# A fused six-block kernel: value copies moved to DVE, two normalisations to ACT, transposes moved ahead of the projection

## The reference

```
x += 0.5*tanh(LN(x) W1 W2 W3 + b);  x += linear_attention(LN(x))     # 16 heads
x += 0.5*tanh(LN(x) W1 W2 W3 + b);  x += 0.5*(real(ifft(fft(LN(x)) w)) + b)
h  = LN(x)                                                         # softmax block
for each of 16 heads:  q, k, v = h Q, h K, h V                      # 64 wide
                       y = softmax(causal(q k^T / 128)) v;  z += y W / 16
x += z;   x += 0.5*(real(ifft(fft(LN(x)) w)) + b)                   # "z" block
```

## Time and profile before

| what | value |
|---|---|
| median of 3 runs (lowest, highest) | 1288.23 us (1285.64, 1289.4) |
| the profiled execution's own time | 1286.5 us |
| its span, first to last instruction | 1284.8 us |
| mean granted clock of PE | 0.990 |
| busy: PE, PEld, DVE, ACT, POOL | 1211.6, 1047.2, 995.5, 1031.6, 591.3 us |
| batch loop | from about 260 us to the end |

### The profile page before, as it was taken

The page is one execution under the profiler, slowest core; times in us unless marked ns, Lnnn a source line. Parts: engine busy times, 40 slices in busy tenths (PEclk is TensorE's granted clock), DMA queues, the critical chain, the costliest instruction groups (busy, mean ns, idle before and its releaser), DMA issues.

```text
span 1284.8 us, 38257 instructions
## 1 busy us (share of the span) xinstructions
PE 1211.6 (94%) x10883; PEld 1047.2 (82%) x10883; DVE 995.5 (77%) x4814; ACT 1031.6 (80%) x3554; POOL 591.3 (46%) x913
## 2 busy tenths in 40 slices
PE   5799977899999999999999999999999999999996
PEld 4688966778788888888888888888888888888885
DVE  6888879877777777777777777777777777777774
ACT  4866657588788888888888888888888888888883
POOL 4722248534444444444444444444444444444442
PEclk9999999999999999999999999999999999999998
DMA  8000000000000000000000000000000000000000
GB/s 218 1 2 0 1 1 1 1 2 2 3 10 0 8 0 8 0 8 0 8 0 8 0 8 0 8 0 8 0 8 0 8 0 8 0 8 0 9 2 17
DMA packets 14444, 11.81 MB, mean 9 GB/s; under 512 B 852, under 2 KB 12664, under 8 KB 14200
## 3 DMA queue, kind: packets, MB, share of 16 engines
q1 hardware_dynamic: 14240, 11.19, 3.2%
q10 hardware_dynamic: 152, 0.00, 0.0%
HBM read 7.00 MB, written 4.19 MB: 9 GB/s over the span
## 4 chain that ended last, share of the span: by engine, by line
PE 70%; ACT 14%; issue 8%; DVE 3%; POOL 2%; DMA 1%; ACTq 1%; SPq 1%; POOLq 0%; DVEq 0%
PE ps L1145 14%; PE ps L1154 9%; ACT pr L799 7%; PE ps L1128 7%; PE ps L1110 5%; PE ps L1097 5%; PE ps L1114 5%; PE ps L1098 4%; PE ps L1099 4%; ACT qk_hi L784 3%; PE ps L975 2%; PE ps L997 2%; ACT pT L808 1%; PE ps L1136 1%; PE ps L1134 1%
## 5 line engine op out<-in xcount | busy, mean ns | idle before, releaser
L799 ACT ACTIVATE pr<-ps,neg_max 128x128 f32<-128x128 f32 (+1 forms) x1024 | 427.7, 435 | 103.3 <-DVE neg_max L536 103.3
L333 POOL TENSOR_TENSOR pr<-pr,rinv 128x256 f32<-128x256 f32 x256 | 157.9, 617 | 539.8 <-DVE rinv L544 539.8
L536 DVE CUSTOM_DVE_ANT_0 ps<-ps,mask 128x128 f32<-128x128 f32 (+1 forms) x1024 | 329.7, 391 | 0.2
L335 POOL TENSOR_TENSOR pr<-pr,rinv 128x512 f32<-128x512 f32 x256 | 266.5, 1041 | 0.0
L551 DVE COPY pT<-ps 128x512 f32<-128x512 f32 x256 | 175.5, 686 | 97.9 <-PE ps L1128 95.5
L799 ACT ACTIVATION_READ_ACCUMULATOR pr<-ps,neg_max 128x1 f32 x1024 | 222.1, 217 | 0.0
L1128 PE MATMUL ps<-ident,pr 128*128 128x128 f32 x1536 | 211.0, 273 | 2.2 <-POOL pr L335 0.9
L1128 PEld LDWEIGHTS ps<-ident,pr 128*128 128x128 f32 x1536 | 179.9, 141 | 20.9 <-POOL pr L335 2.2
L1145 PE MATMUL ps<-pT,space 128*64 128x256 f32 (+1 forms) x2048 | 196.1, 334 | 0.7 <-ACT pT L808 0.5
L1145 PEld LDWEIGHTS ps<-pT,space 128*64 128x64 f32 x2048 | 127.4, 137 | 56.2 <-ACT pT L808 0.8
L1097 PE MATMUL ps<-x_hi,wqk_hi 128*128 128x256 f32 x512 | 168.5, 329 | 2.8 <-issue 2.3
(11 more groups left out here) (187 smaller groups left out, 2659.7 us busy)
## 6 DMA issues: line engine op xcount, KB each, us to landing
out<-x_all SPq DMA_DIRECT2D x16, 256.0 KB, 2.3
x_all<-L_attn_x SPq DMA_DIRECT2D x1, 768.0 KB, 6.2
x_all<-L_attn_x SPq DMA_DIRECT2D x1, 512.0 KB, 4.0
space<-L_attn_Q SPq DMA_DIRECT2D x1, 512.0 KB, 15.3
space<-L_attn_K SPq DMA_DIRECT2D x1, 512.0 KB, 9.5
space<-L_attn_V SPq DMA_DIRECT2D x1, 512.0 KB, 11.3
space<-L_attn_W SPq DMA_DIRECT2D x1, 512.0 KB, 11.7
dft_s<-dft SPq DMA_DIRECT2D x1, 192.0 KB, 2.6
```

The lines of the kernel that those rows point to most:

```text
L333: nc.gpsimd.tensor_tensor(pr[:, buf, :, 0, :], pr[:, buf, :, 0, :], r[:, :, 0:1].to_broadcast([P, 2, P]), ALU.mult)
L335: nc.gpsimd.tensor_tensor(pr[:, buf, :, 1:3, :].rearrange("p h b k -> p h (b k)"), pr[:, buf, :, 1:3, :].rearrange("p h b k -> p h (b k)") ...
L536: last = nc.vector.tensor_tensor_reduce(o, o, mask[:, T - w:T], -1.0, -MASKED, ALU.add, ALU.min, neg_max[:, j, 2 * h + qt:2 * h + qt + 1])
L799: last = nc.scalar.activation(dst, ps[:, BANK_S + 2 * j + h, qt * P:qt * P + w], ACT.Exp, bias=neg_max[:, j, at:at + 1], scale=-1.0, accum ...
```

## The change

- DVE makes the copies of the even turns' value products (`values_copy`: quarter 2 in turn 0, quarter 0 of the next batch in turn 6), with the same semaphore `v_ready`; ACT keeps those of the odd turns.
- ACT makes both normalisations of the batch loop, as `x*rstd + shift`, behind its second pT copy and ahead of the even pair's exponentials; POOL gets two small products for each (-mean and shift), DVE a wait for POOL's shift ahead of the statistics.
- In turn 2 PE makes the transposes ahead of the projection, z's first, and ACT copies x's transpose ahead of `qk_whole`; z's stays behind it. DVE's `x_low` gets a wait for `z_xT_ready` of an earlier batch.
- Ahead of the loop and behind it the same moves are made; the first norm stands ahead of ACT's copies of the q and k weights.

```diff
@@ declarations (rest left out) @@
+        act_pause = sb("act_pause", [P, 3])
+        z_neg = sb("z_neg", [P, BT]); z_shift = sb("z_shift", [P, BT])
+        z_shift_ready = sem("z_shift_ready")
@@ -307,19 +307,17 @@
             def inv_std(n, j, w):
 
                 pool.wait_ge(mv_ready, count(n + 1))
+                if w == GT and above_0(n - 1):
+                    pool.wait_ge(xn_ready, count(n - 1))
                 if above_0(n - 1):
-                    pool.wait_ge(xn_ready, count(n - 1))
-                if w == GT and above_0(n - 1):
                     pool.wait_ge(xn_act_ready, count(n - 1))
-                if w == GT:
-                    nc.gpsimd.tensor_tensor(neg_mean[:, j, :], mv[:, j, :, 0], minus_1[:], ALU.mult).then_inc(neg_mean_ready, 1)
+                nc.gpsimd.tensor_tensor(neg_mean[:, j, 0:w], mv[:, j, 0:w, 0], minus_1[:, 0:w], ALU.mult).then_inc(neg_mean_ready, 1)
                 nc.gpsimd.tensor_tensor(veps[:, j, 0:w], mv[:, j, 0:w, 1], eps_t[:, 0:w], ALU.add).then_inc(pool_step, 1)
                 pool.wait_ge(pool_step, count(n + (POOL0 + 1)))
                 nc.gpsimd.tensor_tensor(rstd[:, j, 0:w], veps[:, j, 0:w], half_neg[:, 0:w], ALU.pow).then_inc(rstd_ready, 1)
-                if w == GT:
-                    pool.wait_ge(rstd_ready, count(n + 1))
-                    pool.wait_ge(neg_mean_ready, count(n + 1))
-                    nc.gpsimd.tensor_tensor(shift[:, j, :], neg_mean[:, j, :], rstd[:, j, :], ALU.mult).then_inc(shift_ready, 1)
+                pool.wait_ge(rstd_ready, count(n + 1))
+                pool.wait_ge(neg_mean_ready, count(n + 1))
+                nc.gpsimd.tensor_tensor(shift[:, j, 0:w], neg_mean[:, j, 0:w], rstd[:, j, 0:w], ALU.mult).then_inc(shift_ready, 1)
 
             def g_inv_std(phase):
                 return lambda g, j: inv_std(g + phase * G, j, GT)
@@ -343,9 +341,12 @@
                 pool.wait_ge(z_mv_ready, count(b + 1))
                 if above_0(b):
                     pool.wait_ge(z_xn_ready, count(b))
+                nc.gpsimd.tensor_tensor(z_neg[:], z_mv[:, :, 0], minus_1[:, 0:BT], ALU.mult)
                 nc.gpsimd.tensor_tensor(z_veps[:], z_mv[:, :, 1], eps_t[:, 0:BT], ALU.add).then_inc(z_veps_ready, 1)
                 pool.wait_ge(z_veps_ready, count(b + 1))
                 nc.gpsimd.tensor_tensor(z_rstd[:], z_veps[:], half_neg[:, 0:BT], ALU.pow).then_inc(z_rstd_ready, 1)
+                pool.wait_ge(z_rstd_ready, count(b + 1))
+                nc.gpsimd.tensor_tensor(z_shift[:], z_neg[:], z_rstd[:], ALU.mult).then_inc(z_shift_ready, 1)
 
             inv_std(SOFT, 0, BT)
             inv_std(SOFT + 1, 1, BT)
@@ -505,14 +506,15 @@
 
 
             def ln_soft_stats(b, j):
+                if above_0(b - 1):
+                    dve.wait_ge(shift_ready, count(b + (SOFT - 1)))
                 stats(b + SOFT, lambda t: xb(b, t, 1), BT, j, 4 * G)
 
-            def ln_soft_norm(b, j):
-                normalise(b + SOFT, lambda t: xb(b, t, 1), BT, j)
-
             def x_low(b, j):
 
                 dve.wait_ge(xhi_ready, count(b + 1))
+                if above_0(b - 2):
+                    dve.wait_ge(z_xT_ready, count(b - 2))
                 nc.vector.tensor_tensor(x_lo[:, j, :], ps[:, BANK_X, 0:T], x_hi[:, j, :].bitcast(F32), ALU.subtract).then_inc(xlo_ready, 1)
 
             def qk_low(n, j):
@@ -551,6 +553,14 @@
                 nc.vector.tensor_copy(pT[:, j].rearrange("p h b q -> p (h b q)")[:, 0:512],
                                       ps[:, BANK_T, :]).then_inc(pTa_ready, 1)
 
+            def values_copy(b, j, c):
+
+                dve.wait_ge(v_done, count(4 * b + (c + 1)))
+                if c == 0:
+                    if above_0(PAIRS * (b - 1)):
+                        dve.wait_ge(pv_done, count(PAIRS * (b - 1)))
+                nc.vector.tensor_copy(vv[:, j, c % 2, 512 * (c // 2):512 * (c // 2) + 512], ps[:, BANK_X, :]).then_inc(v_ready, 1)
+
             def add_z(b, w_after=None):
                 dve.wait_ge(w_done, count(b + 1 if w_after is None else w_after))
                 nc.vector.tensor_tensor(xb(b), ps[:, BANK_X, 0:BT * D], xb(b), ALU.add).then_inc(x_ready, 1)
@@ -562,6 +572,8 @@
 
             def z_stats(b):
                 dve.wait_ge(x_ready, count(b + (SOFT + 1)))
+                if above_0(b):
+                    dve.wait_ge(z_shift_ready, count(b))
                 nc.vector.memset(pause[:, 6:7], 0.0)
                 for t in range(BT):
                     last = nc.vector.bn_stats(z_bst[:, t, :], xb(b, t, 1))
@@ -572,15 +584,6 @@
                     last = nc.vector.bn_aggr(z_mv[:, t, :], z_bst[:, t, :])
                 last.then_inc(z_mv_ready, 1)
 
-            def z_norm(b):
-                dve.wait_ge(z_rstd_ready, count(b + 1))
-                if above_0(b):
-                    dve.wait_ge(z_tr_done, count(b))
-                for t in range(BT):
-                    last = nc.vector.tensor_scalar(z_xn[:, t * D:(t + 1) * D], xb(b, t, 1), z_mv[:, t, 0:1],
-                                                   z_rstd[:, t:t + 1], ALU.subtract, ALU.mult)
-                last.then_inc(z_xn_ready, 1)
-
             def qk_weights_low():
 
                 for i in range(4):
@@ -598,12 +601,10 @@
                                             v_hi[:, 512 * i:512 * i + 512].bitcast(F32), ALU.subtract).then_inc(su_lo, 1)
 
             ln_soft_stats(0, 0)
-            ln_soft_norm(0, 0)
             ln_soft_stats(1, 1)
             qk_weights_low()
             x_low(0, 0)
             v_low()
-            ln_soft_norm(1, 1)
             qk_low(0, 0)
             qk_low(1, 1)
             mask_scores(0, 0)
@@ -613,20 +614,20 @@
                 for p in range(0, PAIRS, 2):
                     n = b * PAIRS + p
                     inv_sum(n, 0)
-                    if p == 0 and above_0(b - 1):
-                        z_norm(b - 2)
                     if p == LN_TURN and has_batch(b + 2):
                         ln_soft_stats(b + 2, jb)
                     if p == Z_TURN and not first:
                         z_stats(b - 1)
                     if p == X_TURN and not last:
                         x_low(b + 1, 1 - jb)
+                    if p == 0:
+                        values_copy(b, jb, 2)
+                    if p == V_TURN and not last:
+                        values_copy(b + 1, 1 - jb, 0)
                     if not (first and p == 0):
                         probs_T(n - 1, 1)
                     if not (last and p == PAIRS - 2):
                         qk_low(n + 2, 0)
-                    if p + 1 == LN_TURN + 3 and has_batch(b + 2):
-                        ln_soft_norm(b + 2, jb)
                     if not (last and p == PAIRS - 2):
                         qk_low(n + 3, 1)
                     if p + 1 == W_TURN + 2 and not first:
@@ -640,12 +641,10 @@
                         mask_scores(n + 3, 1)
 
             batches(dve, batch)
-            z_norm(B - 2)
             probs_T(B * PAIRS - 1, 1)
             add_spectral(B - 2, B)
             add_z(B - 1, B + 1)
             z_stats(B - 1)
-            z_norm(B - 1)
             add_spectral(B - 1, B + 2)
 
 
@@ -756,6 +755,26 @@
                          [(2, xT_out(SPEC1)), (3, act_norm(SPEC1))]],
                    early={0: small_out})
 
+
+            def ln_soft_norm(b, j):
+                act.wait_ge(shift_ready, count(b + (SOFT + 1)))
+                if above_0(b + (SOFT - 1)):
+                    act.wait_ge(tr_done, count(b + (SOFT - 1)))
+                nc.scalar.copy(act_pause[:, j:j + 1], shift[:, j, 0:1])
+                for t in range(BT):
+                    last = nc.scalar.activation(xn[:, j, t * D:(t + 1) * D], xb(b, t, 1), ACT.Identity,
+                                                bias=shift[:, j, t:t + 1], scale=rstd[:, j, t:t + 1])
+                last.then_inc(xn_act_ready, 1)
+
+            def z_norm(b):
+                act.wait_ge(z_shift_ready, count(b + 1))
+                if above_0(b):
+                    act.wait_ge(z_tr_done, count(b))
+                nc.scalar.copy(act_pause[:, 2:3], z_shift[:, 0:1])
+                for t in range(BT):
+                    last = nc.scalar.activation(z_xn[:, t * D:(t + 1) * D], xb(b, t, 1), ACT.Identity,
+                                                bias=z_shift[:, t:t + 1], scale=z_rstd[:, t:t + 1])
+                last.then_inc(z_xn_ready, 1)
 
             def x_high(b, j):
                 act.wait_ge(tr_done, count(b + (SOFT + 1)))
@@ -838,10 +857,12 @@
                     act.wait_ge(w_done, count(b + 1 if w_after is None else w_after))
                 nc.scalar.copy(z_xT[:], ps[:, BANK_X, T:2 * T]).then_inc(z_xT_ready, 1)
 
+            ln_soft_norm(0, 0)
             qk_weights_high()
             x_high(0, 0)
             v_high()
             w_out()
+            ln_soft_norm(1, 1)
             qk_whole(0)
             qk_high_even(0, 1)
             for c in range(2):
@@ -857,16 +878,12 @@
```

(34 more changed lines are left out.)

## The result

Before 1287.99 us (median of 4 runs, 1285.64 to 1289.4), changed 1275.06 us (4 runs, 1270.17 to 1279.25); ratio 0.9901, 95% interval 0.9881 to 0.9921. That is 12.9 us faster; 18 were forecast (1269.5, range 1258 to 1282). Beside other kernels the changed one came out the same again: 1275.37 against 1288.21, ratio 0.9909 (0.9887 to 0.9931). Its profiled execution took 1279.25 us, with a span of 1276.0.

A forecast was written before the change was run, and what follows sets the result against it. PE was taken to bound the batch loop, with ACT and DVE mattering only where PE waits for them. -25.4 - 4.5 + 10.5 + 1.3 = -18.1 us gave 1269.5 us, range 1258 to 1282.

The forecast's parts named there:

- The value copy leaving ACT: First and fourth double turns: PE's wait for ACT's odd exponentials goes wholly, 62 double turns x 0.41 = -25.4 us.
- The copy on DVE covered, 0.35 to spare: Even turns: DVE's 0.68 us value copy fits a hole of DVE, done 0.35 us before PE's next value product.
- The norms on ACT: First and fourth double turns: 0.88 us per norm makes ACT level with PE; costed at nothing inside those turns.
- DVE's relief: Norms leaving DVE free time in which PE waited for nothing: worth nothing.
- Transposes, +10.5: Second double turn: new PE wait for the projection's copy, one bank, 0.35 x 30 batches = +10.5 us (0 to +15).
- x_lo, -4.5: PE's output projection: x_lo ready about 0.6 us earlier, so its 0.15 wait per batch goes, -4.5 us (0 to -4.5).
- Edges, +1.3: Outside the batch loop: +0.9 us for the norm behind the last batch, +0.4 for the first norm ahead, together +1.3.
- A: 62% chance: the forecast as worked out, 1263 to 1277 us.
- B: 12% chance: turn 2 costs nothing, its new wait covered or the wait before paid elsewhere; 1259 us.
- D: 4% chance: slower, ACT's norm stretched by shared access to SBUF; 1310 us at 0.7 more per norm.
- E: 4% chance: DVE reaches the value copy late and PE waits for v_ready; 1285.6 us at 0.6 late.
- C: 18% chance: ACT becomes the bound, each norm costing 0.2 us more than 0.88; 1281.5 us.

The follow-up runs named there:

- DVE's copy twice: The changed kernel with DVE's copy of the even value product made twice, first to unused memory: 1284.7 us, 0.9980 of before.
- The extra scaling: The changed kernel with one more scaling of a tile, to unused memory, behind each norm on ACT: 1295.3 us, 1.0064 of before.
- norms-only kernel: The kernel before with only the two norms of the batch loop moved to ACT: 1301.5 us, 1.0115 of before.
- the kernel with the value copies alone: The kernel before with only the even turns' value copies moved from ACT to DVE: 1267.1 us, 0.9853 of before.
- the better version: The kernel before with even turns' value copies on DVE, both norms left on DVE, z's moved between the low parts: 0.9799, then 0.9808 of before (1264.1 us).

## Why the prediction held, and where its sum was off

- **The value copy leaving ACT** (-25.4). Right in place and size: 0.41 and 0.39 in the two double turns, no PE wait for the exponentials. Value copies alone, with z's norm out of the way, make the whole of the 24.7 to 25.9.
- **The copy on DVE covered, 0.35 to spare.** Right; DVE's copy twice took the reserve and 0.28 more.
- **The norms on ACT, "level with PE", costed at nothing inside their double turns.** Right for the fourth and nearly for the first (ACT 7.10 and 7.13 busy; the two scores of the first lie 0.60 apart, 0.03 more than without a wait), and the price 0.88 was exact. The extra scaling shows how near the edge it was. DVE's relief is worth nothing, as said.
- **Transposes, +10.5.** The mechanism was right, the term too small: 0.46 a batch instead of 0.35 (PE wanted to go 0.66 behind 620.57, at 621.23, and went at 621.69). ACT's lag at the start was as forecast (620.21 - 619.46 = 0.75 against 0.77), and so was the copy's start (1.48 behind the double turn's start; I had 1.53). What failed is "the copy ends 0.59 later": it took 0.70, on an ACT that had worked without a hole since 614.12. That makes 0.06 of the 0.10, as the copy began 0.05 sooner than forecast; the other 0.04 is that PE wanted to go at 1.77 behind the start and not at 1.81. Together 0.10 x 30 = 3 us.
- **x_lo, -4.5.** Wrong step, right size by luck. The step was "x_lo is ready about 0.6 earlier". I had read the new DVE wait as reached long before, and the list of changes calls it a wait for an earlier batch's copy. It is called for batch b + 1, so its count is that of z's copy in this very turn, and the row names it: 1.40 idle until z_xT. x_lo came 2.55 behind the start of the double turn instead of 2.20. PE gained all the same. The last load of the odd turn's projection and the first of the output projection behind it lie 0.32 apart before and 0.18 after (means of 27 batches; 0.12 without a wait). That is 0.14 a batch, some 4 us. It comes from PE, which reaches this place 0.46 later because it has waited for the projection's copy, and not from an earlier x_lo. The wait keeps ACT's and DVE's reads of bank X apart; a version without it wasn't tried.
- **Edges, +1.3.** Right: 0.5 ahead of the loop, and behind it 0.4 more until z's norm starts (POOL) and 0.4 more for the norm itself.
- Together the loop gained 0.49 a batch instead of 0.62: 0.10 less by the transposes, the rest in hundredths by the first double turn and x_lo. That is about 15.2 - 1.3 = 13.9 by the two profiles' batches, and 12.9 by the runs (10.2 to 15.3).
- **Rivals.** 1275.06 lies in A's span, near its upper end. B falls with the wait of 0.44, D with norms that never cost more than 0.88, E as no PE wait for DVE's copy is listed. C, ACT as the bound, was the nearest of them: not as a dearer norm, but through later endings in the second double turn.
- **The rule on adds and products.** The Trainium skill ("ScalarE: Activation LUTs", section "Rules for kernel authors") sends such adds and products to VectorE, with speed in bf16 as its reason. The runs point the same way: with the transposes as before in both, the kernel with its norms on DVE and z's moved has a ratio of 0.9799 to 0.9808, and the one with the norms on ACT 0.9883, about 10 us. The reason here is not a tile's price but ACT's place in the chain. The prediction's comparison of the prices set a distance (0.39) beside lengths (0.32 to 0.62), and its upper length was a tile held up by POOL, as the last section shows. The Trainium skill's same page, section "What ACT_TABLE_LOAD costs", gives an activation with two pointer operands as 186 + 2 x 93 + 0.833 ns per element, and 93 ns of overlap; that makes an estimate of 479 ns for 128 elements. Rows give 486 long and 0.39 from start to start, so the trace agrees.

## What to carry to other kernels

Read a wait as a chain, not as an engine's load: here ACT held PE with a third of a microsecond while it had about 0.9 us free in the same double turn, and moving the one copy that lay inside the chain gave everything. What is moved in exchange has a price only if it lands inside a chain itself, so try the move of the critical piece alone first, and then the order within the engine that takes it. When an added wait carries a batch number, put the call's argument into it before calling it long reached.

## What the runs showed that I had not expected

An ACT instruction's listed time grows in a long stretch without a hole, while the distance from start to start stays. The norms-only kernel, ACT, the same copy of the projection (L776) in two double turns that follow each other, and y's copy (L830) ahead of the second and again after a hole:

```profile
618.14 0.69 ACT L776 COPY qk_raw<-ps 128x512 f32<-128x512 f32 x1
618.64 0.68 ACT L821 COPY space<-ps 128x512 f32<-128x512 f32 x1
...
625.22 0.77 ACT L830 COPY space<-ps 128x512 f32<-128x512 f32 x1
625.69 0.79 ACT L776 COPY qk_raw<-ps 128x512 f32<-128x512 f32 x1
626.17 0.58 ACT L844 COPY z_xT<-ps 128x256 f32<-128x256 f32 x1
...
631.38 0.37 ACT L804 ACTIVATE pr<-ps,neg_max 128x128 f32<-128x128 f32 x1 [1.13 <-DVE neg_max L536]
...
632.98 0.60 ACT L830 COPY space<-ps 128x512 f32<-128x512 f32 x1
```

0.59 The earlier trace rows to 0.79 for a 128x512 copy whose distance hardly moves, 0.50 at 618.14 and 0.48 at 625.69. y's copy went from 0.77 at 625.22 back to 0.60 behind the hole of 1.13. It isn't only how the profile lists it: PE, which waits for the copy's end, went at 621.69, 0.05 behind the listed end of a copy that took 0.70 (620.94). What stretches the end wasn't settled.

The second: a tile of z's norm on DVE took 0.34 to 1.08 us by what POOL did beside it. The kernel before, DVE and POOL:

```profile
643.89 0.62 POOL L333 TENSOR_TENSOR pr<-pr,rinv 128x256 f32<-128x256 f32 x1 [1.12 <-DVE rinv L544]
643.97 1.61 DVE L580 TENSOR_SCALAR z_xn<-x_all,z_mv,z_rstd 128x128 f32 x2 [0.16 <-issue]
644.46 1.04 POOL L335 TENSOR_TENSOR pr<-pr,rinv 128x512 f32<-128x512 f32 x1
```

POOL's second scaling ends at 645.50 and DVE's second tile at 645.58. From 350 to 1200 us, 14 tiles began while POOL did nothing and took 0.33 to 0.34. 27 began within L333 and took 0.61 to 0.64, and 13 within L335 and took 1.08. Each of these 40 ended 0.08 or 0.09 us behind the end of the POOL instruction that it began in. So such a tile isn't slowed in proportion: it ends with POOL's instruction. In the kernel with the value copies alone there are again 13 tiles of 1.08, and behind each of them, 1.73 us after its start, comes one of the 13 PE waits for DVE's copy. In the better version none of the 56 tiles lies beside a POOL instruction, and all take 0.34. No run moved POOL's scaling alone.
